# A transformer-block kernel on one core: the written orders of all five engines within a step are rearranged

## The reference, cut to what matters

```python
q = q * cos + _rotate_half(q) * sin          # the same for k
scores = jnp.einsum('bhqd,bhkd->bhqk', q, k) / jnp.sqrt(jnp.float32(f))
scores = scores + alibi[None]                # and a causal mask
attn = jnp.einsum('bhqk,bhkd->bqhd', softmax(scores), v)
y = jnp.einsum('bshd,hdm->bsm', attn, w_out) + b_out + residual
out = y + bitlinear(silu(bitlinear(y_q, w_gate)) * bitlinear(y_q, w_up), w_down)
```

## Time and profile before

| | |
|---|---|
| median of 3 runs | 1929.69 us (1925.01 to 1931.16) |
| the profiled execution | 1925.48 us, of which its span 1923.7 us |
| instructions | 49050 |
| mean granted TensorE clock | 0.961 |

### The profile page before, as it was taken

How to read it: one execution, slowest core, us unless ns; L and a number is a source line. 1 busy time by engine, 2 the same in 40 slices (tenths; PEclk the granted TensorE clock), 3 DMA queues, 4 the chain that set the end, 5 groups by cost and what they waited for, 6 DMA issues and landing times.

```text
span 1923.7 us, 49050 instructions
## 1 busy us (share of the span) xinstructions
PE 1743.9 (91%) x16742; PEld 1286.5 (67%) x16742; DVE 1448.5 (75%) x4932; ACT 1350.2 (70%) x3808; POOL 1153.0 (60%) x1291
## 2 busy tenths in 40 slices
PE   1755899999999999999999999999999999999975
PEld 1733577677777777777776767777777777776753
DVE  1371687787888888788887888888888888888774
ACT  0112677788777777777788777777777788877763
POOL 0007667666667776667766667766677666666600
PEclk7867999999999999999999999999999999999997
DMA  9402211222222222212222222222122222222200
GB/s 227 159 4 52 54 42 48 62 54 57 57 56 56 62 62 62 53 47 56 62 54 57 56 54 59 62 62 60 47 50 61 57 58 56 55 55 54 56 12 12
DMA packets 98074, 113.75 MB, mean 59 GB/s; under 512 B 22721, under 2 KB 60066, under 8 KB 97570
## 3 DMA queue, kind: packets, MB, share of 16 engines
q1 hardware_dynamic: 97826, 110.61, 22.5%
HBM read 26.62 MB, written 8.42 MB: 18 GB/s over the span
## 4 chain that ended last, share of the span: by engine, by line
PE 48%; DVE 27%; POOL 7%; ACT 6%; issue 6%; SPq 4%; DMA 3%; DVEq 0%; POOLq 0%; ACTq 0%
PE bank L688 24%; PE bank L794 5%; DVE arena L1202 4%; DVE ptr_l L1210 3%; PE bank L783 3%; PE bank L781 3%; DVE arena L1321 3%; PE bank L928 3%; DMA rot<-rq 2%; DVE es L1359 2%; ACT arena L503 2%; PE bank L805 2%; POOL arena L460 2%; POOL rot L456 2%; DVE th L1343 2%
## 5 line engine op out<-in xcount | busy, mean ns | idle before, releaser
L503 ACT ACTIVATE arena<-arena,nm 128x129 f32<-128x129 f32 (+1 forms) x1024 | 456.7, 452 | 142.5 <-DVE nm L1202 139.4
L452 POOL TENSOR_TENSOR arena<-rq,cos 128x256 f32<-128x256 f32 (+1 forms) x384 | 343.4, 908 | 278.3 <-ACT rq L494 278.3
L456 POOL TENSOR_TENSOR rot<-rot,sin 128x512 f32<-128x512 f32 x256 | 324.9, 1269 | 192.2 <-DMA rot<-rq 192.2
L1210 DVE TENSOR_TENSOR ptr_l<-bank,ptr_h 128x384 f16<-128x384 f32 x512 | 279.6, 551 | 178.3 <-ACT ptr_h L513 178.3
L688 PE MATMUL bank<-xt_h,weights 128*128 128x256 f16 x2048 | 382.3, 275 | 12.4 <-ACT rq L494 9.1
L1202 DVE CUSTOM_DVE_ANT_0 arena<-bank,bias 128x129 f32<-128x129 f32 (+1 forms) x1024 | 315.4, 352 | 64.3 <-PE bank L783 49.7
L460 POOL TENSOR_TENSOR arena<-arena,rot 128x256 f32<-128x256 f32 (+1 forms) x384 | 331.5, 877 | 37.3 <-POOL rot L456 0.9
L494 ACT ACTIVATE rq<-bank,bqk 128x256 f32<-128x256 f32 x512 | 214.6, 472 | 168.3 <-PE bank L688 138.5
L688 PE MATMUL bank<-xt_l,weights 128*128 128x256 f16 x1024 | 281.3, 275 | 0.0
L513 ACT ACTIVATE ptr_h<-bank 128x384 f16<-128x384 f32 x512 | 248.3, 485 | 23.9 <-PE bank L794 18.2
L794 PE MATMUL bank<-eye,arena 128*128 128x128 f32 x1536 | 260.0, 282 | 1.7 <-DVE ptr_l L1210 1.5
(11 more groups left out here) (186 smaller groups left out, 3210.4 us busy)
## 6 DMA issues: line engine op xcount, KB each, us to landing
rot<-rq SPq DMA_DIRECT2D x1024, 64.0 KB, 2.0
arena<-in_x SPq DMA_DIRECT2D x4, 2048.0 KB, 18.2
xin<-in_x SPq DMA_DIRECT2D x32, 256.0 KB, 3.1
hr<-hr SPq DMA_DIRECT2D x32, 256.0 KB, 2.4
out<-h SPq DMA_DIRECT2D x64, 128.0 KB, 1.9
arena<-in_L_attn_w_qkv SPq DMA_DIRECT2D x2, 1536.0 KB, 6.5
arena<-in_L_attn_w_out SPq DMA_DIRECT2D x1, 1024.0 KB, 9.9
arena<-in_L_ffn_w_gate SPq DMA_DIRECT2D x1, 1024.0 KB, 6.3
```

Source lines behind the costliest of these rows:

```text
L452: ins = pool.tensor_tensor(dst, rq[:, g % 2, :, cols], cos[:, cols].unsqueeze(1).broadcast_to([P, 2, cols.stop - cols.start]), ALU.mult)
L456: pool.tensor_tensor(r, r, sin[:, :].unsqueeze(1).broadcast_to([P, 2, SIDE]), ALU.mult).then_inc(t2_ready, 1)
L503: act.activation(cols, cols, ACT.Exp, bias=nm[:, t, h:h + 1], scale=-1.0, accum_out=rs[:, t, h:h + 1]).then_inc(e_done, 1)
L1210: tt(ptr_l[:, h % PTR_RING], pt_bank[u % 2][:, 0:3 * P].rearrange("p (b n) -> p b n", b=3), ptr_h[:, h % PTR_RING], ALU.subtract).then_inc ...
```

## The change

The bodies of the five `step` functions get a new order. No call is added or dropped over the whole run and no wait is touched; the place at which a step is cut is moved too, which alone changes nothing, since steps follow on each other. SP and GpSimd:

```diff
@@ SP
             def step(s):
-                rotate(s - 1, 6)
                 load(s + 1)
-                store(s - 3, 1)
-                rotate(s - 1, 7)
-                rotate(s, 0)
-                rotate(s, 1)
                 rotate(s, 2)
                 rotate(s, 3)
                 rotate(s, 4)
                 store(s - 2, 0)
+                store(s - 2, 1)
+                move(s - 1)
                 rotate(s, 5)
-                move(s - 1)
+                rotate(s, 6)
+                rotate(s, 7)
+                rotate(s + 1, 0)
+                rotate(s + 1, 1)
@@ GpSimd
             def step(s):
-                row_operators(s + 1)
+                row_operators(s)
+                add_bias(s - 1)
+                token_rstd(s - 2)
+                rotate(s - 1, 3)
+                image_rstd(s)
+                rotate(s - 1, 4)
+                rotate(s - 1, 5)
+                rotate(s - 1, 6)
+                rotate(s - 1, 7)
                 rotate(s, 0)
-                add_bias(s)
                 rotate(s, 1)
                 rotate(s, 2)
-                rotate(s, 3)
-                token_rstd(s - 1)
-                rotate(s, 4)
-                image_rstd(s + 1)
-                rotate(s, 5)
-                rotate(s, 6)
-                rotate(s, 7)
```

From TensorE's diff, the stretch around the tokens of a block, and the step's last values of an image beside `scores(s - 1, 0)`:

```diff
...
+                attention_out(s - 1, 1)
                 values(s - 1, 2)
+                attention_out(s - 1, 2)
                 transposes(s - 1, 4)
-                attention_out(s - 1, 1)
-                values(s - 1, 3)
-                attention_out(s - 1, 2)
                 project(s, 4)
                 transposes(s - 1, 5)
+                values(s - 1, 3)
                 scores(s - 1, 4)
+                synthesise(s + 1)
                 transposes(s - 1, 6)
                 values(s - 1, 4)
-                synthesise(s + 1)
                 turn_tokens(s - 1)
-                scores(s - 1, 5)
                 out_transposes(s - 1, 0)
...
```

279 lines of the change are left out of this document (140 added, 139 removed).

## The result

The changed kernel takes 1883.42 us (median of 4 runs, 1882.49 to 1884.51) where the kernel before takes 1928.30 beside it (4 runs, 1925.01 to 1931.16): ratio 0.9768, 95% interval 0.975 to 0.9786. That is 44.9 us less. The forecast was 1905.3 with a range from 1892: the sign was right, the gain was nearly twice the forecast, and outside the range.

What follows compares the result with a forecast made beforehand. TensorE was taken to bound the kernel. 30 steps at 1.0 less (-30.0), fill +4.7 and drain +0.9 gave -24.4 against the profiled 1925.48; set against the median 1929.69, 1905.3 us, own range 1892 to 1918, 1892 to 1936 with (a).

Steps and rivals of the forecast that it cites:

- the last line of the sum: Whole run: the profiled execution lies 4.2 below the median 1929.69; the same difference gives 1905.3.
- What bounds the kernel: Steady step of 52.31 us: TensorE, matmuls busy 91%, has no room; the others have some 10 us each.
- The wait before turn_tokens: Steady step: token_scales at +5.2 instead of +5.56, turn_tokens at +7.4, its wait 0.1 in place of 0.93.
- at two only: Old order: TensorE waits only before turn_tokens (0.93) and project_v (0.20), by starts 1.35 a step together.
- Neighbours: 0 to 0.3 gained, I take 0.15: Steady step: five scores-transposes pairs vanish, 0.05 each; two more values stand before scores, 0.1 each.
- What is late next: Steady step: new waits for weights_lo at out_transposes 0 (0.3) and transposes 7 (0.25), 0.65 to 0.7 in sum.
- Fill, +4.7: Start: row_operators(1) between rotations costs 2.9, image_rstd(1) idles some 3.4, less 1.6 from landed copies; bounds +2 and +8.
- Drain, +0.9 with the attention of image 31 at 0: End: inner_peak 2 behind gate_up 3 costs +0.9; attention of image 31 unpriced, 0, bounds -4 and +4.
- (b): Four rotations before scores(c + 1, 0), cover 0.2: a late copy makes the step 53.6, 1974 us; chance 0.12.
- (c): Clock: long pauses every step bring TensorE's lower clock, 53.3 a step, some 1965 us; chance 0.02.
- (a): About five edges with 0.1 to 0.2 room slip by 0.2 each, eating the gain; some 1929 us; chance 0.14.
- (d): Steps lose all waits, 1.4 a step gained, 1893 us; counted within the forecast, together chance 0.72.

Runs made afterwards that it cites:

- a1: Kernel before, GpSimd alone: token_rstd moved ahead of rotation 3 and image_rstd ahead of rotation 4; 1895.50 us, ratio 0.9837.
- g1: Kernel before, orders untouched, without the addition of 1e-5 to both variances (L1245); 1919.22 us, ratio 0.9962.
- k1: a1 with two VectorE swaps: values_lo 2 ahead of evict_scores 15, weights_lo 3 ahead of evict_scores 6; 1902.70 us, ratio 0.9878.
- e3: Changed kernel; for blocks 31 and 32 alone, inner_peak 2 and 3 directly behind gate_up 2 and 3; 1880.25 us, ratio 0.9767.
- f1: Changed kernel with token_rstd ahead of add_bias, early inner_peak for blocks 30 to 32, row_operators(1) ahead of rotation 0; 1878.60 us, ratio 0.974.
- d1: Changed kernel with synthesise put back behind transposes 6 and values 4 on TensorE; 2082.71 us, ratio 1.0801.
- c1: a1 with three TensorE moves: values 3 behind transposes 5, values 14 ahead of transposes 15, values 12 ahead of project_v 3; 2018.96 us, ratio 1.0485.

## Why the prediction was wrong

The forecast lay 21.9 us above the measurement. The 30 steps make 20.7 of it, and the two ends together take 2.0 back. Another 3.3 come from the last line of the sum: the changed kernel's profiled execution lies 0.9 below its median, not 4.2.

**What bounds the kernel: right.** TensorE before and after; the rule of the Trainium skill ("Perfetto Trace Analysis", section Identifying the Most-Contended Engine) would still see room in it (weight loads busy 38.3 of 50.7 us), and its listed waits come to 9.8 us in 1450.

**The wait before turn_tokens: right in size and in its main cause.** Forecast 1.0 by starts; a1 alone takes 0.9 of it away by two swaps on GpSimd. I had priced residual at 4.4 us and took that for its length: 0.8 of it, and 0.67 in the mean, was VectorE held up at L1245. g1 puts that share at 0.28 a step, since the rest of the hold was behind the queue. So token_scales came at +4.55 in an undisturbed step, not at +5.2; with the steps in which the new order brings the hold back its mean is +5.11.

**Waits "at two only", "nearly nothing else": this step failed, and it is the larger part of the miss.** The prediction let the new order give back the two listed waits, 1.35 by starts, and took every other old edge at nothing. By starts the old order lost 2.75 us a step. At the two listed calls it was 1.45. Some 1.0 lay where the prediction had nothing: 0.70 in five calls (attention_out 1, transposes 10, values 10, down 0, values 14), the rest in pieces of at most 0.06 of which it isn't settled what they are. They are shorter than the modelled ends of matmuls, so absent from the list on which I built. That they are waits is shown for attention_out 1 (k1). For down 0 and values 14 the same kind of call between the same kinds of neighbours took 0.12 and 0.14 less elsewhere (down 1 in the changed kernel, values 5 in the one before). For the others it is argued from their being gone after.

**"Neighbours: 0 to 0.3 gained, I take 0.15": right in kind, half the size.** The five pairs measure 0.055 each, 0.28. The loss set against it, values standing before scores at 0.1 each, isn't there: every call costs 0.09 more ahead of scores, whichever it is, and there are eight scores in both orders.

**"What is late next", 0.68: wrong in places, too small in size.** No wait at out_transposes 0 or transposes 7. Instead values 4 waits for normalise 0, an edge I missed (transposes 6, 0.36), project_v 0 behind values 9 costs 0.27 (one of the five edges I had called tight), row_operators 0.13 at scores 4; with what is smaller, 1.13. Net, in place of the -0.82 that the terms give and the -1.0 that I took: -2.75 + 1.13 = -1.62 a step for images 3 to 28, and -1.69 over all 30.

**Fill, +4.7: the mechanism right, the size wrong.** Its mechanism came as described, GpSimd in the changed kernel:

```profile
166.71 0.21 POOL L421 COPY op_now<-ops 128x32 f32<-128x32 f32 x1
...
169.25 0.29 POOL L430 TENSOR_TENSOR s<-s 128x64 f32<-128x64 f32 x1
...
177.68 0.69 POOL L442 TENSOR_TENSOR rstd<-ve,negh 128x2 f32<-128x2 f32 x1 [3.07 <-DVE ve L1245]
```

row_operators(1) takes 2.8 between two rotations and image_rstd(1) waits 3.07 (forecast 2.9 and 3.4), and project(0, 0) to scores(0, 0) grew by 3.4. In that stretch the forecast was +4.7. But a gain was missed, and the mark has moved. normalise_image(0) ran beside row_operators(1) before and took 2.16 us, now 0.73; from the end of synthesise(0) to project(0, 0) it is 6.3 us instead of 8.1 (another 0.4 is that this execution began earlier). And from scores(0, 0) to scores(1, 0) it is 52.4 instead of 54.5, of which 1.6 are calls that lie on the other side of the marks now.

**Drain, +0.9 with the attention of image 31 at 0: wrong.** +8.6, of which 2.9 are the calls behind the mark; the 5.7 that are left are outside the bound of 4 too. An order made for the steady step puts calls of the next image between a wait and what it waits for, and at the end that cover is missing; e3 shows it for the peaks. The last block's +0.9 was right in kind (0.7 between turn_tokens(32) and the end). Of the first 4.5, up to attention_out(31, 2), 2.3 are calls that moved into that stretch. In it the granted clock was 0.92 where it was 1.00 before, and the listed waits 3.4 us where they were 2.0. In f1, with block 30's early peaks, the clock stayed at 1.00 and the stretch was 1.4 shorter, with waits of 3.2: so the 1.4 goes with the clock, which is argued and not isolated. With the 2.9 that e3 took, some 1.2 of the 8.6 is left, and its cause is open.

**The rivals.** (b), four rotations: scores(c + 1, 0) waited once in 1450 us (0.6), so the cover of 0.2 held. (c), the clock, did not come, but d1 shows it: behind pauses of 1.33 and 1.80 us the clock was at its lower level for most of 4.5 us. (a): of its five tight edges one slipped, by 0.27; what it missed is that the old order itself lost about 1.0 a step at such edges. (d), all waits lost, 1.4 a step, was nearest, and I put it inside the forecast rather than beside it.

## What to carry to other kernels

Measure idle time of a bounding engine from start to start of its calls against the shortest length seen of each, not by the list of waits alone: here 1.1 of 2.75 us a step was listed. Then compare the same call behind different neighbours before calling the rest waits: 0.28 wasn't. And when an order moves, check that a mark between stretches still has the same work on each side. An instruction whose length varies between its executions is itself a finding; look at what the other engine runs as it ends. A tight order is a whole: one move of synthesise cost 200 us. Of the small moves tried by themselves, GpSimd's two swaps kept their gain (31 us); two swaps on VectorE, which has some 10 us of room a step too, didn't (k1).

## What the hardware showed

GpSimd holds VectorE up until its own instruction is through. L1245, an addition on 128x2 that takes 0.17 us, was long in 25 of its 55 executions from 300 to 1750 us of the kernel before (up to 1.28 us), and each time it ended 24 to 30 ns behind the end of a GpSimd instruction that had started before it. L1335 was long in 56 of 56 in the changed kernel, and ended 144 to 156 ns behind the end of one. L1210 and L1234 (one input from PSUM) and the reduction L1252 were never long, though GpSimd was at work beside most of them. The other way round little is seen: 28 of GpSimd's multiplications with sin (1.27 us) started 0.19 us before L1335 ended in the changed kernel, and took 1.31 to 1.32. The Trainium skill ("SBUF — State Buffer", section Who interferes with whom) says that VectorE in a mode that uses both ports, which tensor_scalar can enter, and GpSimd share a pair of ports, that whoever issues first has it for the whole instruction, and that the other fully blocks. The trace agrees where GpSimd is first, and shows that two columns are enough to be caught; that L1245 and L1335 are in such a mode isn't to be seen in it.

TensorE's granted clock was lower behind some of its pauses: 0.50 for most of the 4.5 us behind pauses of 1.33 and 1.80 us (d1). Not behind every one: in the kernel before, with pauses of up to 1.5 us before turn_tokens, it was 1.00 from 300 to 1750 us, and in c1, with pauses of 2.2 us in nearly every step, 0.99 in the mean.
